# Two sets of transposes exchanged on the tensor engine near the end of a four-layer conditioned residual stack, with one copy moved on ScalarE

## The reference

```python
x = x + L0(x, cond)          # batch-scaled down/up projection, relu
x = x + L1(x, cond)          # per-batch low-rank weight, rank 30
x = x + L2(x, cond)          # modulated projection, 16-head attention inside each token, modulated projection
x = x + L3(x, ids, states)   # see below

# L3, the layer whose end is touched
def _ln(x, g, b): return (x - mean) * rsqrt(var + 1e-5) * g + b
h = _ln(_ln(x, pw_g[ids], pw_b[ids]), cp_g[c], cp_b[c])
t = _ln(x, tm_g[c], tm_b[c]);  s = _ln(x, ms_g[k], ms_b[k])
m, n, r = x + vector_per_batch            # three of these
cat = concat(w0*h, w1*t, w2*m, w3*n, w4*r, w5*s)
out = _ln(silu(cat @ W1 + b1) @ W2 + b2, g, b)
```

## Time and profile before

| | us |
|---|---|
| median of the runs | 471.96 |
| the runs | 471.39, 471.96, 484.14 |
| the profiled execution, its own time | 471.39 |
| its span in the profile | 469.6 |
| mean granted PE clock, share of full speed | 0.971 |

### The profile page before, as it was taken

The page is one execution under the profiler, slowest core; times in us unless marked ns, Lnnn a source line. Parts: engine busy times, 40 slices in busy tenths (PEclk is TensorE's granted clock), DMA queues, the critical chain, the costliest instruction groups (busy, mean ns, idle before and its releaser), DMA issues.

```text
span 469.6 us, 9298 instructions
## 1 busy us (share of the span) xinstructions
PE 419.7 (89%) x3740; PEld 253.9 (54%) x3740; DVE 349.1 (74%) x649; ACT 276.8 (59%) x413; POOL 176.1 (38%) x149
## 2 busy tenths in 40 slices
PE   3899986959899899999999999989998989998992
PEld 2586554534545554555554564555555547644781
DVE  0477889596847995699759984898389867886755
ACT  0200688974777865796588649784878568702110
POOL 4004999076333244133413152314241243237124
PEclk9999897997999999999999999999999999998997
DMA  5994337616291428441662358142904392333002
GB/s 130 384 302 159 69 114 227 151 36 210 49 254 60 135 65 219 126 135 51 167 193 90 96 138 222 46 140 46 268 8 130 95 254 62 82 104 89 2 0 89
DMA packets 68486, 61.03 MB, mean 130 GB/s; under 512 B 53646, under 2 KB 55314, under 8 KB 68059
## 3 DMA queue, kind: packets, MB, share of 16 engines
q1 hardware_dynamic: 64139, 43.90, 34.2%
q0 software_dynamic: 3728, 12.59, 8.4%
q10 hardware_dynamic: 576, 3.95, 2.1%
HBM read 39.30 MB, written 21.13 MB: 129 GB/s over the span
## 4 chain that ended last, share of the span: by engine, by line
PE 58%; ACT 18%; DVE 13%; DMA 4%; issue 3%; SPq 2%; POOL 1%; POOLq 0%; DVEq 0%
PE ph L842 21%; ACT bd L1372 7%; PE pk L809 6%; PE pp L851 3%; PE pp L792 3%; PE pk L832 3%; PE ph L995 3%; ACT vc L1366 3%; ACT bd L1359 3%; PE pk L800 2%; PE pp L974 2%; DMA bd<-in_w_dec 2%; PE pp L823 2%; PE pk L725 2%; PE ph L725 1%
## 5 line engine op out<-in xcount | busy, mean ns | idle before, releaser
L1372 ACT ACTIVATE bd<-vc,ownrow 128x512 f32<-128x512 f32 x116 | 73.3, 710 | 0.0
L1359 ACT ACTIVATE bd<-kc,ownrow 128x512 f32<-128x512 f32 x112 | 70.5, 710 | 0.3
L485 POOL TENSOR_TENSOR demod<-demod,neghalf 128x32 f32<-128x32 f32 x8 | 44.5, 5576 | 36.2 <-DVE demod L1700 36.2
L809 PE MATMUL pk<-bd,et 128*32 128x128 f32 x1024 | 33.0, 283 | 3.5 <-ACT et L1376 2.6
L809 PE MATMUL pk<-bd,kc 128*32 128x128 f32 x1024 | 31.1, 274 | 3.2 <-ACT bd L1359 3.2
L809 PEld LDWEIGHTS pk<-bd,kc 128*32 128x32 f32 x1024 | 27.0, 110 | 12.6 <-ACT bd L1359 8.0
L809 PEld LDWEIGHTS pk<-bd,et 128*32 128x32 f32 x1024 | 28.4, 114 | 9.1 <-issue 5.0
L792 PE MATMUL pp<-ys,kwT 128*128 128x512 f32 x64 | 29.4, 602 | 0.0
L842 PE MATMUL ph<-x2T,w 128*128 128x512 f32 x56 | 27.4, 634 | 0.0
L842 PE MATMUL ph<-hnT,w 128*128 128x512 f32 x56 | 27.0, 627 | 0.0
L842 PE MATMUL ph<-tT,w 128*128 128x512 f32 x56 | 25.9, 605 | 0.2 <-DVE tT L2165 0.2
(11 more groups left out here) (447 smaller groups left out, 936.8 us busy)
## 6 DMA issues: line engine op xcount, KB each, us to landing
xin<-in_x SPq DMA_DIRECT2D x8, 512.0 KB, 5.3
x_dram<-x SPq DMA_DIRECT2D x8, 512.0 KB, 2.6
k_dram<-kxb SPq DMA_DIRECT2D x16, 256.0 KB, 3.3
kt<-k_dram SPq DMA_DIRECT2D x8, 512.0 KB, 4.1
v_dram<-kxb SPq DMA_DIRECT2D x8, 512.0 KB, 5.0
vt<-v_dram SPq DMA_DIRECT2D x8, 512.0 KB, 6.1
av_dram<-av SPq DMA_DIRECT2D x8, 512.0 KB, 4.8
attnT<-av_dram SPq DMA_DIRECT2D x8, 512.0 KB, 4.4
```

Source lines behind the costliest of these rows:

```text
L485: gp.tensor_tensor(q, q, neghalf[:, 0:4 * CB].rearrange("p (l a b) -> p l a b", l=2, a=2), ALU.pow).then_inc(gs_dem, 1)
L809: ins = mm(pk[32 * r:32 * r + 32, o:o + 128], weights(h, 4 * i + r)[:, 16 * pair:16 * pair + 32], bd[:, h, 8 * i + 2 * r + pair, :], start ...
L1359: fn(bd[:, h, :, 16 * b:16 * b + 16].rearrange("p (q z) x -> p q z x", z=2), kc[:, 16 * h:16 * h + 16, :].rearrange("p q (z x) -> p q z x" ...
L1372: fn(bd[:, h, :, 16 * b:16 * b + 16], vc[:, SH * h:SH * h + SH, :], ACT.Copy, scale=ownrow[:, 1, b:b + 1]).then_inc(s, 1)
```

## The change

On PE in `step_d7`, the eight transposes of `x2T` into `P23`, with their two waits, now stand ahead of the eight transposes of `h1_prev` into `pk`. On DVE in `step_d7`, the statistics on `P23` stand ahead of the product that makes `hnT`. On ACT in `step_v7`, the copy of `P23` to `xin`, with its two waits, stands ahead of the second half of the attention output's copy to `av`. No instruction is added or removed, and POOL's and SP's lists are as they were.

```diff
@@ step_d7 of PE @@
                 hidden(10, xnT, p_hs)
-                after(pe, v_hn, e, 4)
-                after(pe, v_o, min(e + 1, NC - 1))
-                turn(pk, h1_prev, p_hnT)
                 after(pe, v_x2, d, 2)
                 after(pe, v_sT, d - 1)
                 for j in range(NT):
...
                         ins = tr(P23[:, q:q + 128], x2T[:, f, 128 * j:128 * j + 128], ident[:, :])
                 ins.then_inc(p_x2k, 1)
+                after(pe, v_hn, e, 4)
+                after(pe, v_o, min(e + 1, NC - 1))
+                turn(pk, h1_prev, p_hnT)
                 after(pe, g_oh, d)
                 after(pe, v_hT, d - 1)
                 gain(P01, D, p_tg)
@@ step_v7 of ACT @@
                 outputs_out(1, a_osb1)
-                after(act, p_back1, v)
-                outputs_back(1, a_av1)
                 after(act, p_x2k, d)
                 after(act, v_mv[0], d, 4)
                 fn(xin[:, :, :], P23.rearrange("p (j f) -> p j f", j=NT), ACT.Copy).then_inc(a_x2k, 1)
+                after(act, p_back1, v)
+                outputs_back(1, a_av1)
@@ step_d7 of DVE @@
                     stt(x2T[:, f, :], tmp_o[:, f, :], cols[:, 6 + f:7 + f], x1r[:, f, :], ALU.add, ALU.add).then_inc(v_x2, 1)
+                after(ve_, p_x2k, d)
+                for j in range(NT):
+                    ve_.bn_stats(stats[:, 0, j, :], P23.rearrange("p (j f) -> p j f", j=NT)[:, j, :]).then_inc(v_bn[0], 1)
+                after(ve_, v_bn[0], d, NT)
+                settled(ve_)
+                for j in range(NT):
+                    ve_.bn_aggr(mv[:, 0, j, :], stats[:, 0, j, :]).then_inc(v_mv[0], 1)
                 after(ve_, a_hnT, e)
                 after(ve_, p_cg, e)
                 tt(hnT[:, :, :], hnT[:, :, :], halves(P01), ALU.mult).then_inc(v_hT, 1)
-                after(ve_, p_x2k, d)
...
-                    ve_.bn_aggr(mv[:, 0, j, :], stats[:, 0, j, :]).then_inc(v_mv[0], 1)
                 after(ve_, g_rs[0], d)
                 after(ve_, a_x2k, d)
```

More of the change, by code:

```diff
@@ L2197, in step_d7 @@
                     stt(x2T[:, f, :], tmp_o[:, f, :], cols[:, 6 + f:7 + f], x1r[:, f, :], ALU.add, ALU.add).then_inc(v_x2, 1)
-                after(ve_, a_hnT, e)
-                after(ve_, p_cg, e)
-                tt(hnT[:, :, :], hnT[:, :, :], halves(P01), ALU.mult).then_inc(v_hT, 1)
                 after(ve_, p_x2k, d)
@@ L2207, in step_d7 @@
                     ve_.bn_aggr(mv[:, 0, j, :], stats[:, 0, j, :]).then_inc(v_mv[0], 1)
+                after(ve_, a_hnT, e)
+                after(ve_, p_cg, e)
+                tt(hnT[:, :, :], hnT[:, :, :], halves(P01), ALU.mult).then_inc(v_hT, 1)
                 after(ve_, g_rs[0], d)
```

## The result

The changed kernel took 475.5 us, the median of 20 runs, against 472.24 for the kernel before. The ratio is 1.0063, with a 95% interval of 1.0037 to 1.0090. That is 3.0 us (1.8 to 4.2) more. The profiled execution took 472.91, with a span of 471.1.

The account below looks back on a forecast made before the run. PE was taken to bound the kernel. 1.9 us of later resumption less 0.6 from the clock is 1.3 on 471.39, 472.7; half of the 0.6 to the median added gives 473.0 us, range 471.0 to 474.9.

Parts of the forecast that it names:

- PE bounds the place, and nothing behind 434 swallows a loss: PE, 434.13 to 456.00 us: busy for all 21.87 us, so any loss at 428 reaches the end in full.
- The late attention load, sized at 0.3 us: ACT copy in step_v7: load of `attnT` issued 0.65 us later, so DVE starts, and `x2T` ends, 0.3 us late.
- the upper bound: Late `attnT` load: at most 0.65 us, if it shares the DMA engines with the output store and keeps no slack.
- The exchange, sized at 1.6 of the 1.9 us: PE and DVE in step_d7: PE resumes at 430.12 in place of 428.22, 1.9 us later, including the load's 0.3.
- the 0.63 for `x2T` and the 2.46 in the stop: Expected in PE's profile: 0.6 to 1.0 us idle before the `x2T` transposes, about 2.5 before the table values.
- the statistics are hidden: DVE in step_d7: statistics run during ACT's copy to `hnT`, leaving DVE free 0.04 us after ACT is done.
- the earlier variance has no use: Chunk 7's variance on DVE comes at 428.73 against 429.93, but POOL is adding into `xin` until 430.58.
- The clock gives back 0.6: PE behind the stop: slow clock meets 2.4 us of work, not 3.4, costs 1.3 us and gives back 0.6.
- The rival in which the clock stays up, 471.4 and no loss: PE's eight products behind the stop take 3.44 us, not 5.33; time as before, 471.4 us; chance 0.14.
- The rival in which the clock stays low longer: Clock at half through all of PE's last products: 2.9 us more, 474.3, or 474.9 from the median; chance 0.18.
- That the slow stretch cost the kernel before 1.9 us: PE's eight products at 428.81 took 5.33 us against 3.44 at full clock, read as a cost of 1.9 us.

Follow-up runs that it names:

- the second execution: The changed kernel traced once more, nothing altered; 65.03 us from the start of PE's products on chunk 6's `x2T` to the end of the span.
- the kernel with the later store: Changed kernel with POOL's output store of chunk 5 moved from step_v7 behind chunk 6's reciprocal root in step_d7; 65.49 us from PE's chunk 6 `x2T` products to the end.
- the two covered kernels: Kernel before and changed kernel, each with eleven unread transposes in PE's stop; 61.75 and 63.33 us from PE's chunk 6 `x2T` products to the end.

## Why the prediction was wrong

The mechanism and the sign were right. Two terms of the sum failed: the late load was sized too small, and the clock gave nothing back. Forecast were 1.0 us more for the median, which was called no change, and 1.3 for one execution; measured were 3.0 and 2.76. The measured median lies 0.6 us above the range, the median of the runs that the ratio uses, 474.5, just inside it; it is the size of the change that the sum had wrong.

- **PE bounds the place, and nothing behind 434 swallows a loss.** Right: PE is busy for all of 21.79 us behind the products, as it was. Only with the clock up is there a wait ahead of 434 in the kernel before, for chunk 7's norm, and this one does swallow a part.
- **The late attention load, sized at 0.3 us.** This step failed. It cost 1.0: line 2175 starts 10.10 us behind the anchor and not 9.10. The 0.7 us of later issue was as I said. But I took the landing time of 4.0 as given, "measured in the same company", and the company changed. The same edit lets DVE finish the output sooner (line 2160 starts 2.80 us behind the anchor and not 3.12), which the prediction had noted as a gain of nothing. So POOL's store goes 0.69 us ahead of the load, where it had been 0.36 us behind. With the store away the load takes 3.5 and DVE does not wait. The sum is 0.73 of later issue and 0.6 of longer transfer, less the 0.4 of slack. I had named that sharing in the upper bound and then set the bound at 0.65, which is the later issue alone.
- **The exchange, sized at 1.6 of the 1.9 us.** Right: 1.73 by itself, with the 0.63 for `x2T` and the 2.46 in the stop that I gave as marks. It was also right that the statistics are hidden, and that the earlier variance has no use; with DVE's order put back the resumption moves by nothing.
- **The clock gives back 0.6.** This step failed too. It assumed that the clock falls at the moment at which it fell before. It fell later, some 25 us behind the anchor and not 21.7, and the products took 5.33 us again; they were as slow in the second execution. In seven of the eight executions with slow products behind the stop it fell 0.5 to 1.5 us after PE had resumed, in either order, and in the eighth, the kernel with the later store, 0.4 us ahead of that; why there, no run shows. Nothing came back. The terms thus are 1.0 + 1.7 - 0 = 2.7, not 1.3.
- **The rival in which the clock stays up, 471.4 and no loss.** Wrong in its price. The kernel before had 0.5 us to gain from the same luck, and the late load stays: the two covered kernels are 1.6 apart, and the changed one with the clock up is still 1.1 above the kernel before with its slow products. The forecast held the changed kernel's good case against the old one's bad case.
- **The rival in which the clock stays low longer.** Seen once, in the kernel with the later store, at 6.42 us for the products.
- **That the slow stretch cost the kernel before 1.9 us.** Wrong: 0.5 (62.24 to 61.75). I took the longer products for the loss, and did not ask what was late next. Chunk 7's norm was, at 431.95 + 1.38 = 433.33, 1.1 us behind the time at which fast products would have ended. Its row in the kernel before:

```profile
431.95 1.38 DVE L2211 TENSOR_SCALAR xn<-x2k,mv,rstd 128x256 f32<-128x256 f32 x4 [2.02 <-POOL rstd L651]
```

Not shown is how often the clock falls behind the stop in either kernel. Of the executions with a trace the kernel before did it in both and the changed one in both.

## What to carry to other kernels

When an edit delays one transfer and speeds up its neighbour, look at which of the two is issued first afterwards: the landing time read from the trace holds only for the old order. When a slow stretch covers a wait, its price is not the extra time of its instructions but the distance to the next late thing. A stop of the bounding engine is better filled with work that it has anyway than rearranged, but only if the engine that feeds it keeps up: sixteen products moved into the stop were worth 2.0 us together with an earlier affine on DVE, and nothing without it (one execution), while the exchange of two sets of transposes made PE resume 1.7 us later.

## What the runs showed of the hardware

- PE's granted clock does not follow the length of a stop alone. Behind the stop of 1.59 us the eight products were slow (about 5.4 us) in three executions of the kernel before and its variants and fast (3.70) in two. Behind the stop of 2.46 us they were fast once, slow four times, and once slow from the table values on (6.42).
- With eleven transposes of float32 in the stop, whose result nobody reads, the clock stayed up in three executions out of three, and with products in the stop also in three out of three; without either it stayed up in three of eleven.
- A 512 KB load from DRAM took 3.5 us alone, 3.7 to 4.0 with a 512 KB store issued 0.4 us behind it, and 4.6 with that store issued 0.7 us ahead.
- One 128x256 float32 instruction on DVE took 2.44 us in place of 0.40 while POOL ran a tensor_tensor from and to SBUF; in the kernel before the same POOL instruction ran beside DVE's four statistics instructions, which read PSUM, and these took their usual 1.41 in all, and beside the four that make mean and variance from SBUF, which took their usual 0.38.
